# Gated Flamingo block on one core: query norms moved from the rotated queries into the scale of ScalarE's exponentials

## What is computed

```python
qkv = x @ Wqkv
q, k, v = jnp.split(qkv, 3, -1)            # 16 heads of 64
q = l2norm(q) * qs
k = l2norm(k) * ksc
q = q * cos * scale + rotate_half(q) * sin * scale
k = k * cos * inv + rotate_half(k) * sin * inv
# windows of 32 tokens; each sees its own and the one before, masked
sim = jnp.einsum('bhwie,bhwje->bhwij', bq, bk2) * 8.0
attn = jax.nn.softmax(jnp.where(mask, -big, sim), -1)
out = jnp.einsum('bhwij,bhwje->bhwie', attn, bv2)
x = out.reshape(b, n, 1024) @ Wo + x
x = ffn_layer(shift_tokens(x), ...) + x    # layer norm, W1, gelu gate, W2
```

## Time and profile before

| what | value |
|---|---|
| median of 3 runs | 2158.55 us (2143.49 to 2164.61) |
| the profiled execution | 2149.13 us |
| its span, first to last instruction | 2147.3 us |
| TensorE busy | 1939.6 us (90%) |
| VectorE busy | 1570.1 us (73%) |
| ScalarE busy | 1072.3 us (50%) |
| GpSimd busy | 888.4 us (41%) |
| mean granted TensorE clock | 0.945 |

### The profile page before, as it was taken

The page is one execution under the profiler, slowest core; times in us unless marked ns, Lnnn a source line. Parts: engine busy times, 40 slices in busy tenths (PEclk is TensorE's granted clock), DMA queues, the critical chain, the costliest instruction groups (busy, mean ns, idle before and its releaser), DMA issues.

```text
span 2147.3 us, 84750 instructions
## 1 busy us (share of the span) xinstructions
PE 1939.6 (90%) x35408; PEld 1309.3 (61%) x35408; DVE 1570.1 (73%) x3156; ACT 1072.3 (50%) x1879; POOL 888.4 (41%) x1167
## 2 busy tenths in 40 slices
PE   6777775799999999999999999999999999999996
PEld 3444442466676666666766676767676766676664
DVE  4545435668787878787878787878787878787873
ACT  2333322346464656454646465646465655564653
POOL 0000001446454545454645464535454646454540
PEclk8778776899999999999999999999999999999997
DMA  1000101546565656565656565655665556654551
GB/s 64 5 10 5 54 1 19 79 75 88 81 104 104 99 82 89 81 111 104 86 82 86 104 102 94 86 81 94 110 95 86 85 84 110 106 84 75 88 83 32
DMA packets 73330, 166.84 MB, mean 78 GB/s; under 512 B 16592, under 2 KB 23504, under 8 KB 72400
## 3 DMA queue, kind: packets, MB, share of 16 engines
q0 software_dynamic: 36864, 100.71, 35.0%
q1 hardware_dynamic: 36432, 65.68, 12.4%
HBM read 20.57 MB, written 1.05 MB: 10 GB/s over the span
## 4 chain that ended last, share of the span: by engine, by line
PE 56%; DVE 14%; DMA 14%; issue 10%; POOL 4%; ACT 2%; POOLq 0%; DVEq 0%; SPq 0%; ACTq 0%
PE ps L957 14%; DMA big<-big 13%; PE ps L992 8%; PE ps L1016 5%; PE ps L968 5%; PE ps L897 4%; PE ps L1029 4%; PE ps L1046 3%; POOL big L454 3%; DVE big L771 3%; PE ps L877 2%; DVE big L802 2%; DVE big L779 2%; DVE big L789 2%; PE ps L1059 2%
## 5 line engine op out<-in xcount | busy, mean ns | idle before, releaser
L454 POOL DMA_DIRECT2D big<-big x768 | 606.1, 1490 | 70.7 <-DVE big L771 60.3
L957 PE MATMUL ps<-big,wn_sb 128*128 128x256 f32 x1536 | 398.4, 396 | 24.4 <-issue 14.9
L525 ACT ACTIVATE big<-ps 128x512 f32<-128x512 f32 x384 | 228.8, 596 | 339.4 <-PE ps L957 333.0
L957 PEld LDWEIGHTS ps<-big,wn_sb 128*128 128x128 f32 x1536 | 276.0, 192 | 103.4 <-issue 46.8
L779 DVE TENSOR_TENSOR big<-big,ps 128x512 f32<-128x512 f32 x384 | 243.5, 681 | 99.7 <-DMA big<-big 50.5
L538 ACT ACTIVATE big<-ps 128x512 f32<-128x512 f32 x192 | 114.6, 597 | 367.1 <-PE ps L992 367.1
L784 DVE TENSOR_REDUCE top<-ps 128x8 f32<-128x512 f32 x192 | 123.3, 684 | 203.2 <-PE ps L1016 203.2
L768 DVE TENSOR_TENSOR big<-ps,tab 128x512 f32<-128x512 f32 x384 | 257.9, 682 | 12.3 <-ACT big L525 12.3
L771 DVE TENSOR_TENSOR big<-ps,tab 128x512 f32<-128x512 f32 x384 | 257.7, 681 | 0.0
L445 POOL TENSOR_TENSOR big<-big 128x512 f32<-128x512 f32 x96 | 121.7, 1268 | 300.5 <-ACT big L542 300.5
L1100 PE MATMUL ps<-big,wo_sb 128*128 128x256 f32 x768 | 214.1, 382 | 0.0
(11 more groups left out here) (146 smaller groups left out, 3142.6 us busy)
## 6 DMA issues: line engine op xcount, KB each, us to landing
big<-big POOLq DMA_DIRECT2D x768, 128.0 KB, 4.9
big<-big SPq DMA_DIRECT2D x96, 256.0 KB, 3.7
big<-big SPq DMA_DIRECT2D x96, 192.0 KB, 3.8
wn_sb<-in_wn SPq DMA_DIRECT2D x6, 1024.0 KB, 8.8
wn_sb<-in_wn SPq DMA_DIRECT2D x6, 512.0 KB, 4.8
wo_sb<-in_wo SPq DMA_DIRECT2D x6, 512.0 KB, 3.2
w_sb<-in_w SPq DMA_DIRECT2D x6, 341.0 KB, 3.0
w_sb<-in_w SPq DMA_DIRECT2D x6, 192.0 KB, 3.0
```

Of the source, the lines that this page charges most:

```text
L454: eng.dma_start(rot[to:to + 32, at:at + 4, :], src[32 * r:32 * r + 32], accum_op=ALU.add).then_inc(added[i], 16)
L525: eng.activation(sq[:, two, :], ps[:, i % 2, :].rearrange("p (a t) -> p a t", a=2), ACT.Square).then_inc(sq_d, 1)
L957: mm = eng.matmul(ps[:, k % 2, a * T:a * T + T], wn_sb[:, u * P:u * P + P], sT, start=True, stop=True)
```

## The change

The queries are no longer multiplied by their norms. `H` falls from eight pieces to four (keys only, `hat` halves), `R` from eight to four. The scores are computed from `rot` (queries) and `hat` (keys). Since a query's norm is one number per row of a score tile, it becomes a per-partition scale: TensorE's new step `Q` transposes the norms `n_r` with two matmuls and ScalarE's new step `q` copies them to `rq`. Each exponential is now `exp(score * rq + shift)`. It can take one head and one tile of 128 tokens only, so the two instructions of 128 x 1024 become 32 of 128 x 64, eight in each of `x0` to `x3`, read straight from PSUM. VectorE's `D` shrinks from a subtraction over 128 x 512 to the product `shift = -max * rq` over 128 x 8. The banks of the scores are now free only when the exponentials have been taken, so `S1` waits for `x1` and `W0` for `x3`. A constant factor moves into the rotary table. The four lists are reordered.

```diff
-        HATS = [i // 2 + PAIRS // 2 * (i % 2) for i in range(PAIRS)]
+        HATS = [PAIRS // 2 + i for i in range(PAIRS // 2)]
...
         PE_PLAN = [(x_[0], int(x_[1:])) for x_ in """
-            S0 k0 k1 F1 S1 k2 k3 T0 g0 T1 F2 k4 k5 W0 W1 g1 g2 k6 T2 k7 U0 T3 g3 W2 W3 U1 F4 O0 O1 O2 U2 O3 U3
-            F5 R0 R1 O4 R2 O5 R3 O6 R4 F6 R5 R6 O7 F7 R7 V0 V1 V2 V3""".split()]
+            S0 k0 F1 k1 k2 g0 F2 k3 S1 k4 T0 g1 k5 k6 g2 T1 k7 T2 W0 g3 W1 T3 F4 U0 W2 W3 U1 Q0 F5 O0 O1 O2 U2
+            O3 U3 F6 O4 R0 O5 R1 F7 R2 O6 R3 O7 V0 V1 V2 V3""".split()]
         ACT_PLAN = [(x_[0], int(x_[1:])) for x_ in """
-            s0 s1 x0 F1 s2 s3 t0 F2 t1 s4 s5 x1 s6 t2 s7 u0 t3 F3 n0 u1 F4 u2 u3 F5 v0 v1 v2 v3""".split()]
+            s0 x0 s1 F1 x1 s2 s3 F2 s4 x2 s5 t0 x3 s6 s7 t1 F3 t2 n0 t3 F4 u0 q0 u1 F5 u2 u3 v0 v1 v2 v3""".split()]
         DVE_PLAN = [(x_[0], int(x_[1:])) for x_ in """
-            X0 X1 D0 D1 c0 c1 d0 d1 X2 X3 D2 c2 d2 c3 d3 D3 Z0 f0 c4 d4 c5 d5 f1 Y0 f2 c6 f3 Z1 n0 d6 c7 Y1 N1
-            d7 N2 N3 N4 N5 N6 H0 H1 H2 F5 H3 H4 F6 H5 H6 H7 F7 e0""".split()]
+            X0 D0 X1 c0 d0 D1 c1 d1 c2 d2 c3 X2 D2 d3 c4 d4 X3 D3 c5 d5 f0 f1 f2 c6 f3 Z0 n0 Y0 N1 N2 Z1 c7 d6
+            d7 Y1 N3 F5 N4 N5 N6 F6 H0 H1 H2 H3 e0 F7""".split()]
         POOL_PLAN = [(x_[0], int(x_[1:])) for x_ in """
-            A0 F0 Z0 m0 Z1 m1 m2 m3""".split()]
+            A0 F0 Z0 m0 m1 Z1 m2 m3""".split()]
...
                     if kind == "x":
-                        eng.wait_ge(sub_d, it * 4 + (2 * i + 2 - 4))
-                        chunk = pr_[:, i, :, :]
-                        eng.activation(chunk, chunk, ACT.Exp).then_inc(ex_d, 1)
+                        c, r = divmod(i, 2)
+                        eng.wait_ge(sub_d, it * 4 + (i + 1 - 4))
+                        for g in range(8):
+                            at = 32 * (g // 2) + 2 * c + r
+                            eng.activation(pr_[:, c, g, KW * r:KW * r + KW], ps[:, 5 + r, KW * g:KW * g + KW], ACT.Exp,
+                                           bias=shift[:, c, r, g:g + 1], scale=rq[:, g % 2, at:at + 1]).then_inc(ex_d, 1)
+                    if kind == "q":
+                        eng.wait_ge(rq_t, it + 1)
+                        if Bh:
+                            eng.wait_ge(sub_d, it * 4)
+                        eng.activation(rq[:, :, :].rearrange("p n d -> p (n d)"), ps[:, 2, 0:T], ACT.Copy).then_inc(rq_d, 1)
...
-                        eng.tensor_tensor(pr_[:, c, :, KW * r:KW * r + KW], ps[:, 5 + r, :].rearrange("p (g k) -> p g k", g=8),
-                                          top[:, c, r, :].rearrange("p (g k) -> p g k", k=1).to_broadcast((P, 8, KW)),
-                                          ALU.subtract).then_inc(sub_d, 1)
+                        if i == 0:
+                            eng.wait_ge(rq_d, it)
+                        norms = rq.rearrange("p t (q m) -> p q t m", m=32)[:, :, :, 2 * c + r]
+                        eng.scalar_tensor_tensor(shift[:, c, r, :].rearrange("p (q t) -> p q t", t=NT),
+                                                 top[:, c, r, :].rearrange("p (q t) -> p q t", t=NT), -1.0, norms,
+                                                 ALU.mult, ALU.mult).then_inc(sub_d, 1)
...
+                def turn_norms():
+                    eng.wait_ge(nchain, it * 4 + 2)
+                    for n in range(NT):
+                        mm = eng.transpose(ps[:, 2, n * P:n * P + P], n_r[:, n * P:n * P + P], ident)
+                    mm.then_inc(rq_t, 1)
...
                 def score(c):
...
                     else:
-                        eng.wait_ge(sub_d, it * 4 + (2 - 4))
-                        eng.wait_ge(hat_d, it * PAIRS)
+                        eng.wait_ge(ex_d, it * 32 + (16 - 32))
+                        eng.wait_ge(hat_d, it * 4)
+                        eng.wait_ge(added[2], it * 64)
...
                 def weigh(q):
                     eng.wait_ge(ptev, it * 4 + (q + 1 - 4))
                     if q == 0:
-                        eng.wait_ge(sub_d, it * 4)
+                        eng.wait_ge(ex_d, it * 32)
```

More of the change, by code:

```diff
@@ L59, in shape_constants @@
     other = np.arange(P) ^ 32
-    rot = np.stack([8.0 * both(cq), 8.0 * both(sq)[other], both(ck), both(sk)[other]], 1).astype(f)
+    rot = np.stack([2048.0 * both(cq), 2048.0 * both(sq)[other], both(ck), both(sk)[other]], 1).astype(f)
     q, k = np.arange(WIN)[:, None], np.arange(KW)[None, :]
@@ L182, in gated_flamingo @@
         rot = view(UNITS * T, UNITS, T)
-        hat = view(UNITS * T, UNITS, T)
+        hat = view(PAIRS * T, PAIRS, T)
         pr_ = view(2 * 2 * 512, 2, 8, 2 * KW)
@@ L205, in gated_flamingo @@
         top = sb("top", [P, 2, 2, 8])
+        shift = sb("shift", [P, 2, 2, 8])
+        rq = sb("rq", [P, NT, P])
         den = sb("den", [P, 2, 2 * 8])
@@ L239, in gated_flamingo @@
                              "wo_d", "x_d", "w_go", "s_go", "vf_free", "y2_d", "den_h", "den_s"))
+        rq_t, rq_d = sem("rq_t"), sem("rq_d")
         chain, nchain, nmid = sem("chain"), sem("nchain"), sem("nmid")
@@ L438, in body @@
                     if kind == "Z":
-                        eng.wait_ge(ex_d, it * 2 + (i - 1))
+                        eng.wait_ge(ex_d, it * 32 + (16 * i + 16 - 32))
                         if A:
@@ L518, in body @@
             def body(b, it, l, A, Bh, F, first):
-                for kind, i in share(ACT_PLAN, A, Bh, F, "snv", "xtu", "F"):
+                for kind, i in share(ACT_PLAN, A, Bh, F, "snqv", "xtu", "F"):
                     if kind == "s":
@@ L766, in body @@
                         eng.wait_ge(sq_d, it * PAIRS + (i + 1))
+                    if kind == "c" and Bh and i in (0, 4):
+                        eng.wait_ge(sc_d, it * 2 + (i // 4 - 1))
                     if kind == "c":
@@ L774, in body @@
                         two = slice(2 * HATS[i], 2 * HATS[i] + 2)
-                        eng.wait_ge(rb, it * PAIRS + (i + 1))
+                        eng.wait_ge(rb, it * 4 + (i + 1))
                         eng.wait_ge(added[ORDER.index(two.start) // 4], it * 64 + 64)
-                        if Bh and i % 4 == 0:
-                            eng.wait_ge(sc_d, it * 2 + (i // 4 - 1))
-                        eng.tensor_tensor(hat[:, two, :], rot[:, two, :], ps[:, i % 2, :].rearrange("p (a t) -> p a t", a=2),
+                        if Bh and i % 2 == 0:
+                            eng.wait_ge(sc_d, it * 2 + (i // 2 - 1))
+                        eng.tensor_tensor(hat[:, 2 * i:2 * i + 2, :], rot[:, two, :], ps[:, i % 2, :].rearrange("p (a t) -> p a t", a=2),
                                           ALU.mult).then_inc(hat_d, 1)
@@ L962, in head_sums @@
                     if g == 0 and Bh:
-                        eng.wait_ge(ss_d, it)
+                        eng.wait_ge(rq_d, it)
                         eng.wait_ge(x_d, it - 1 + FREE)
@@ L977, in spread @@
                     else:
-                        eng.wait_ge(hat_d, it * PAIRS + (n - 1))
+                        eng.wait_ge(hat_d, it * 4 + (n - 1))
                     for a in range(2):
@@ L986, in values @@
                     if j < 2:
-                        eng.wait_ge(hat_d, it * PAIRS + (7 + j))
+                        eng.wait_ge(hat_d, it * 4 + (3 + j))
                     else:
@@ L998, in score @@
                         eng.wait_ge(on_d, it * 4 + (FREE - 4))
-                        eng.wait_ge(hat_d, it * PAIRS - 4)
-                    else:
-                        eng.wait_ge(sub_d, it * 4 + (2 - 4))
-                        eng.wait_ge(hat_d, it * PAIRS)
+                        eng.wait_ge(hat_d, it * 4 - 2)
+                        eng.wait_ge(added[0], it * 64)
+                    else:
+                        eng.wait_ge(ex_d, it * 32 + (16 - 32))
+                        eng.wait_ge(hat_d, it * 4)
+                        eng.wait_ge(added[2], it * 64)
                     eng.sem_inc(s_go, 1)
@@ L1016, in score @@
                                 mm = eng.matmul(ps[WIN * w:WIN * w + WIN, 5 + r, KW * g + skip:KW * g + KW],
-                                                hat[rows, p, at:at + WIN], hat[rows, PAIRS + p, at - WIN + skip:at + WIN],
+                                                rot[rows, p, at:at + WIN], hat[rows, p, at - WIN + skip:at + WIN],
                                                 start=False, stop=False, skip_group_check=True)
@@ L1022, in turn_weights @@
                     if q % 2 == 0:
-                        eng.wait_ge(ex_d, it * 2 + (q // 2 - 1))
+                        eng.wait_ge(ex_d, it * 32 + (16 * (q // 2) + 16 - 32))
                     if q >= 2:
@@ L1097, in project_out @@
                         if A:
-                            eng.wait_ge(ss_d, it + 1)
+                            eng.wait_ge(rq_d, it + 1)
                     eng.wait_ge(oev, it * 4 + (p // 2 + 1 - 4))
@@ L1104, in body @@
```

(6 more changed lines are left out.)

## The result

The changed kernel takes 2224.51 us, the median of 4 runs (2223.28 to 2227.47), against 2157.7 of the kernel before (four runs); the ratio is 1.032, with a 95% interval of 1.027 to 1.037. The forecast was 2214 us, so slower, and it was right. The profiled execution took 2223.28 us, 74 us more than the 2149.13 before.

A forecast was written before the change was run, and what follows sets the result against it. The chain `S0`, rotary stage to `d7`, `m3`'s DMAs, last `H`, values was taken to bound. Pass 35.8 to 37.0 us, 1.2 over 48 passes, is +58: 2207 on the profiled execution, 2214 as median; range 2100 to 2300.

The forecast's parts named there:

- The price of the exponentials: ScalarE: 32 exponentials of 128x64, 378 ns each at pitch 0.28 us, cost 9.0 us against 2.0 now.
- the two columns: ScalarE's small exponentials: bias and scale columns together add 181 ns to each.
- The 0.33 estimated from the Trainium skill: ScalarE's small exponentials: the skill page's costs give pitch 0.33, a pass 1.6 us longer than the forecast's own sum.
- The walk through the pass: Full pass timed step by step from `S0`: `d7` ends at 25.1, `V0` at 33.05, pass 37.0 us.
- the landing, with TensorE close by: Pass end: `m3`'s keys land at 32.2, `V0` follows at 33.05; TensorE's rival path ends at 32.8.
- My 8.3 us from `F5` to `V0`: TensorE, late in the pass: matmuls from `F5` through `O7` take 8.3 us, ending at 32.8.
- VectorE's slack: VectorE has 7 us of slack per pass, so most of the 4.1 us net saved is worth nothing.
- The gain from fewer `H` and `R`: Pass end: three `H` between the landing and `V0` become one, gaining 0.6 us.
- Rival 1: ScalarE's exponentials are cheap: pitch 0.19, pass 34.1 us, time 2075; breaks even at pitch 0.24; chance 0.22.
- rival 4: TensorE's clock falls during waits: three microseconds at half speed cost 1.5 us per pass, about 2286; chance 0.12.

The follow-up runs named there:

- a_no_m3: Changed kernel without the four DMAs of `m3` and `H`'s wait for them (last keys lack their rotated half): 2216.8 us, ratio 1.030.
- b_nq_new_order: Kernel before with the queries' norms left out (four `H`, four `R`), in the changed kernel's list order, without `Q` and `q`: 2140.1 us, ratio 0.993.
- a_scale_only: Changed kernel with exponentials taking the scale column alone, no bias; row maxima computed but unused: 2114.7 us, ratio 0.984.
- a_old_order: Changed kernel's instructions in the list order of the kernel before: 2891.5 us, ratio 1.346.
- a_no_max: Changed kernel without row maxima `X` and without `D`, exponentials with the scale column only: 2113.4 us, ratio 0.983.
- a_no_columns: Changed kernel with constant scale and no bias in the exponentials, query norms and maxima left out of the result: 2108.1 us, ratio 0.980.
- b_no_max: Kernel before without `X` and `D`, four exponentials of 128x512 straight from PSUM: 2264.9 us, ratio 1.052.
- b_no_max_new_order: Kernel before without `X` and `D`, four 128x512 exponentials from PSUM, in the changed kernel's list order: 2190.7 us, ratio 1.016.

## Why the prediction was right

- *The price of the exponentials* was right, pitch 0.28 against 0.289. The pitch was built from a duration of 378 ns and an overlap of 0.10; they measure 460 ns and 0.17, and the two misses cancel. Of its parts, the two columns were right (0.18 forecast, 0.16 to 0.18 measured: 0.289 against 0.105 to 0.134 without any). The 0.33 estimated from the Trainium skill (ScalarE: Activation LUTs, section What ACT_TABLE_LOAD costs) was too long by 0.04.
- *The walk through the pass* was right and a little short at each piece, in us after `S0`: `S1` at 8.8, measured 9.1; `s4` 11.7 against 12.1; `n0` over at 21.8 against 22.3 (1159.94); `d7` over at 25.1 against 25.7 (1163.36); the keys landed at 32.2 against 32.1; `V0` at 33.05 against 33.7; the pass 37.0 against 37.33.
- *The step that failed* is "the landing, with TensorE close by". I had the DMAs of `m3` ending the pass at 33.05 and TensorE's matmuls at 32.8. a_no_m3 shows that the landing doesn't bind, and the chain shows TensorE gapless from `x3`'s end. Also, I let TensorE's path begin with `F4`'s Gelus; it begins 6 us earlier, with `T2`, which waits for `x3`. My 8.3 us from `F5` to `V0` was right (1163.01 to 1171.34), but `F5` starts at 25.4, not at 24.5. So the sum came out near the time by some luck: the path that I took to bind and the one that does stood 0.25 us apart in it.
- *VectorE's slack* was read too broadly. Its 7 us of a pass lie behind `d7`: in the windows of the kernel before it is busy 20.05 of the 21.40 us from 1120.00 to 1141.40. b_nq_new_order shows that VectorE's work can still count there.
- *The gain from fewer `H` and `R`* was right for the old order (0.6 forecast, 0.6 measured). For the new one it stays open; 2 us is the most that these runs suggest.
- *Rival 1* had its breaking point at a pitch of 0.24. At 0.20 the kernel did turn faster (a_scale_only), 2115 where I had 2075 for 0.19. I hadn't priced TensorE's floor, which holds 84% of the chain there.
- *The clock* of rival 4 didn't fall in the changed kernel (1.00 in the pass); a_old_order shows what it looks like where waits are 5 us long.

The sum, by runs: 2.5 us a pass are lost to the second column (a_scale_only), and without any column the pass would be 34.6. What is gained comes from `H`, `R` and `D`. That the two make up 1.55 to 1.9 us exactly was not shown; the pieces were measured in different surroundings.

**The better version** is a_scale_only or a_no_max, which compute the same function 1.6 to 1.7% faster than the kernel before and 5% faster than the changed one. It holds as long as unshifted scores don't overflow. Here queries and keys are normalised, so an unmasked score is at most 8 times the product of the largest learned scales.

## What to carry to other kernels

Before work is moved to an engine that looks half idle, look which of its results others wait for: 7 us more of small activations made the pass 1.55 to 1.9 us longer here, though ScalarE had been 50% busy. Splitting one activation into sixteen changes its price from columns to instructions and operands; the pitch per instruction, with each pointer operand in it, is the number to have. And where a PSUM bank is freed by another engine than before, the matmuls behind that wait must be reordered with it, or the wait costs more than the work.

## What had not been expected

- An exponential of 128x64 without columns costs little. In a_no_columns what follows a group of eight starts 0.84 us (1133.53 to 1134.37) or 1.07 us (1135.11 to 1136.18) after the group, which makes a pitch of 0.105 or 0.134. So small activations are cheap until they carry columns: 0.105 to 0.134 us with none, 0.20 with one (2.31 becomes 1.58 for eight) and 0.29 with two.
- Waits of about 5 us on TensorE cost more than themselves: behind its two, 10.6 us in sum, the pass of a_old_order has 36.9 us of busy matmuls where the changed kernel has 34.8, at a mean clock of 0.90.
- Less work made a kernel slower by 5% (b_no_max), once ScalarE instead of VectorE freed the banks in an unchanged order; the changed order brought back 74 of the 112 us (b_no_max_new_order).
